# Gate scores carried by the residual's transposes, and expert outputs accumulated by DMA, in a convolution-attention and mixture-of-experts block

## What is computed

```python
t = t + ffn(ln_t(t))                       # t: (batch, 3136 tokens, 96)
# ffn(x):
scores = einsum('bsd,de->bse', x, gate_w) + gate_b
probs  = softmax(scores)
masked = probs * (top 2 of probs);  masked = masked / (sum(masked) + 1e-9)
h = gelu(einsum('bsd,edh->ebsh', x, w1) + b1)      # hidden 384
y = einsum('ebsh,ehd->ebsd', h, w2) + b2
out = einsum('bse,ebsd->bsd', masked, y)
```

## Time and profile before

| | us |
|---|---|
| three runs | 895.98, 898.64, 900.95 |
| median | 898.64 |
| span of the profiled execution | 894.8 |
| rest(0), 77 to 190 | PE busy 84.0 of 113.0 |
| round 1, 190 to 392 | PE 183.2, DVE 164.7 of 202.0 |
| round 2, 392 to 597 | PE 180.8, DVE 159.3 of 205.0 |
| round 3, 597 to 781 | PE 166.7, DVE 119.5 of 184.0 |
| last experts, 781 to 894.8 | PE 105.2, ACT 97.7 of 113.8 |

### The profile page before, as it was taken

One profiled execution on the slowest core, in us unless ns is written; L12 is line 12 of the kernel. 1 busy time (PEld: TensorE's weight loads), 2 busy tenths in 40 slices (PEclk: granted clock), 3 DMA queues, 4 the chain that ended last, 5 costly groups with the idle time before them and its releaser, 6 DMA issues.

```text
span 894.8 us, 10704 instructions
## 1 busy us (share of the span) xinstructions
PE 775.4 (87%) x3304; PEld 514.3 (57%) x3304; DVE 670.5 (75%) x1397; ACT 396.8 (44%) x726; POOL 322.5 (36%) x184
## 2 busy tenths in 40 slices
PE   2899779759997898988997798989996998999996
PEld 1454445645664456655664455755663556588885
DVE  6789769899896487878896587899882354667775
ACT  2322412424555107542555106544542134599995
POOL 2000700007777001127677002148897011234443
PEclk9998979559998899998999799999997996999998
DMA  9103401201232001261132001151422000221111
GB/s 179 44 0 108 108 1 54 55 34 39 91 103 79 7 4 36 82 160 39 60 127 83 8 0 39 47 133 42 148 72 78 0 25 16 87 70 55 62 55 31
DMA packets 17312, 55.12 MB, mean 62 GB/s; under 512 B 5008, under 2 KB 8720, under 8 KB 15216
## 3 DMA queue, kind: packets, MB, share of 16 engines
q1 hardware_dynamic: 12656, 39.90, 15.8%
q10 hardware_dynamic: 1536, 9.84, 3.3%
q0 software_dynamic: 3072, 4.82, 2.1%
HBM read 35.07 MB, written 14.65 MB: 56 GB/s over the span
## 4 chain that ended last, share of the span: by engine, by line
PE 51%; DVE 23%; POOL 11%; issue 7%; ACT 3%; DMA 3%; DVEq 0%; ACTq 0%; SPq 0%; POOLq 0%
PE py L615 10%; POOL big L1215 8%; PE pd L555 7%; DVE query L919 6%; PE pa L430 4%; PE ph L470 4%; PE pd L535 3%; POOL x L1225 3%; PE pd L578 3%; PE ph L630 3%; PE ph L631 2%; PE ph L632 2%; DVE key_area L919 2%; DVE big L919 2%; PE ph L653 2%
## 5 line engine op out<-in xcount | busy, mean ns | idle before, releaser
L1225 POOL TENSOR_TENSOR x<-x,ye 96x448 f32<-96x448 f32 x112 | 240.1, 2144 | 464.8 <-DVE ye L1143 461.3
L830 ACT ACTIVATE hid<-ph,b 128x448 f32<-128x448 f32 x252 | 159.0, 633 | 263.8 <-PE ph L632 261.0
L615 PE MATMUL py<-hid,w 128*96 128x448 f32 x504 | 241.0, 560 | 31.5 <-DVE ye L1143 24.4
L630 PE MATMUL ph<-x_hi,w_hi 96*128 (+1 forms) x252 | 169.7, 673 | 0.0
L1143 DVE SCALAR_TENSOR_TENSOR ye<-py,b,gate_all 96x448 f32<-96x448 f32 x112 | 75.3, 677 | 53.0 <-PE py L615 25.3
L615 PEld LDWEIGHTS py<-hid,w 128*96 128x96 f32 x504 | 82.1, 168 | 55.8 <-DVE ye L1143 16.6
L1215 POOL DMA_INDIRECT big<-value_table,rows x64 | 77.3, 1208 | 88.4 <-DMA value_table<-xT 69.2
L631 PE MATMUL ph<-x_lo,w_hi 96*128 (+1 forms) x252 | 94.8, 376 | 0.0
L632 PE MATMUL ph<-x_hi,w_lo 96*128 (+1 forms) x252 | 94.3, 374 | 0.0
L919 DVE SCALAR_TENSOR_TENSOR big<-xpad,conv_w,big 96x3136 f32<-96x3136 f32 (+1 forms) x28 | 90.0, 3215 | 4.7 <-issue 4.3
L919 DVE SCALAR_TENSOR_TENSOR query<-xpad,conv_w,query 96x3136 f32<-96x3136 f32 (+1 forms) x28 | 93.1, 3324 | 0.5
(11 more groups left out here) (136 smaller groups left out, 1089.8 us busy)
## 6 DMA issues: line engine op xcount, KB each, us to landing
gate_all<-gate_rows SPq DMA_DIRECT2D x56, 336.0 KB, 3.1
value_table<-xT ACTq DMA_DIRECT2D x8, 1176.0 KB, 7.2
xs<-in_x SPq DMA_DIRECT2D x4, 1176.0 KB, 8.5
x<-in_x SPq DMA_DIRECT2D x4, 1176.0 KB, 7.9
x<-x SPq DMA_DIRECT2D x4, 1176.0 KB, 6.9
out<-x SPq DMA_DIRECT2D x28, 168.0 KB, 2.0
big<-value_table,rows POOLq DMA_INDIRECT x64
big<-in_w SPq DMA_DIRECT2D x1, 576.0 KB
```

Source lines behind the costliest of these rows:

```text
L615: nc.tensor.matmul(py[e % 2][0:C, 0:GPIX], w2[:, c, :], hid[:, k % 3, :], start=(j == 0), stop=(j == CPE - 1)).then_inc(hid_used, 1)
L630: nc.tensor.matmul(bank, w1_hi[:, cols], xh[:, px], start=True, stop=False)
L830: nc.scalar.activation(hid[:, k % 3, :], ph[k % 2][:, 0:GPIX], ACT.Gelu, bias=b1[:, k % NCH:k % NCH + 1]).then_inc(hid_act, 1)
L1225: ins = p.tensor_tensor(r, r, ye[:, e, :], ALU.add)
```

## The change

1. **Scores with the transposes.** In `x1T` PE multiplies each tile of the residual by `ident_gate`, the identity with four more columns: `gate_w` less the mean of each of its columns. So a tile comes out as 96 channels and 4 raw scores (400 columns a bank instead of 384). The 112 matmuls L578 go. DVE makes the scores with two small operations (`rstd`, then `gate_b`) right behind the normalisation.
2. **Split of the normalised tokens.** `x1c` goes to the two DVE banks `pd`; ACT copies a bank to the high part, DVE subtracts it from the same bank for the low part and so frees the bank. The copy through `xc` and the cast L1083 go. The token tensor of this stage is no longer `xT` but lies in `big`.
3. **Expert outputs.** POOL issues an accumulating DMA (`x1 += ye`) for each output in place of the addition, and waits until it has landed before the next.
4. **Order.** `x1c` no longer has chunks between its groups, `exp` and `gateT` come earlier in the table, `normalise_off` runs with `no_turn`, and the loops of PE, ACT and DVE over rounds 1 and 2 are written out.
5. At the start, PE multiplies `gate_w` by a matrix of 1/96, and DVE subtracts.

```diff
-ROUND = [..., ("x1c", 66, 4, 12), ("score", 71, 0, 13),
-         ("exp", 74, 0, 4), ("gateT", 79, 0, 9), ("offc", 79, 0, 0), ("offs", 82, 0, 0), ...
+ROUND = [..., ("x1c", 66, 0, 12), ("exp", 70, 0, 0), ("gateT", 77, 0, 12), ("offc", 79, 0, 0), ("offs", 82, 0, 0), ...
-              ("x1c", 67, 2, 10), ("score", 72, 3, 10), ("exp", 77, 0, 4), ("gateT", 82, 0, 6), ("end", 84, 0, 1)]
+              ("x1c", 67, 0, 10), ("exp", 70, 0, 0), ("gateT", 78, 0, 12), ("end", 84, 0, 1)]
@@ PE, head
+                nc.tensor.matmul(py[0][0:C, 0:EXPERTS], mean_of, gate_w[:, :], start=True, stop=True).then_inc(gate_mean, 1)
@@ PE, rest
-                    transposes(bank, [x[:, (GRP * g + k) * TP:(GRP * g + k + 1) * TP] for k in range(GRP)], C, TP).then_inc(act_full, 1)
+                    for k in range(GRP):
+                        last = nc.tensor.matmul(bank[0:TP, k * XC:(k + 1) * XC], x[:, (GRP * g + k) * TP:(GRP * g + k + 1) * TP], ident_gate[:, :], start=True, stop=True)
+                    last.then_inc(act_full, 1)
...
-                channels_back(b, "x1c", x1_normed, x1_normed_act, before_x1c)
-                for g in range(NG - 3, NG):
-                    if g == NG - 1:
-                        chunks_to(plan.at("score"))
-                    last = scores(g)
-                last.then_inc(dve_full, 1)
+                for g in range(NG):
                     chunks_to(plan.at("x1c", g))
+                    ...
+                    bank = dve_bank(b, "x1c", g)
+                    transposes(bank, [x1T[:, GRP * g + k, 0:C] for k in range(GRP)], TP, C).then_inc(dve_full, 1)
@@ PE, ACT, DVE
-            with pe.Fori(0, BATCH - 2) as b:
+            for b in range(BATCH - 2):
@@ ACT, x1c
-                    empty(b, "x1c", g, xc[:, g * GPIX:(g + 1) * GPIX], C, GPIX)
+                    i, full = dve_job(b, "x1c", g)
+                    act.wait_ge(dve_full, full)
+                    nc.scalar.activation(xh[:, half(b) + g * GPIX:half(b) + (g + 1) * GPIX], pd[i][0:C, 0:GPIX], ACT.Copy).then_inc(x_high, 1)
@@ DVE, rest
+                link(v.tensor_tensor(sc[:, :, :], x1T[:, :, C:XC], full(rstd[0:TP, :]), ALU.mult))
+                link(v.tensor_tensor(sc[:, :, :], sc[:, :, :], gate_b..., ALU.add))
+                link(v.tensor_reduce(mx[:, :], sc[:, :, :], AX.X, ALU.max))
+                v.tensor_tensor(sc[:, :, :], sc[:, :, :], full(mx), ALU.subtract).then_inc(score_ready, 1)
                 if with_head:
                     dve.wait_ge(x1_normed_act, (b + 1) * (NG - NORM_DVE))
-                    normalise_off(b + 1, turn)
+                    normalise_off(b + 1, no_turn)
@@ DVE, split_x
-                        dve.wait_ge(act_done, acted(b, "x1c", g))
-                        link(v.tensor_copy(xh[:, to], xc[:, px]))
-                        v.tensor_tensor(xl[:, to], xc[:, px], xh[:, to].bitcast(f32), ALU.subtract).then_inc(x_split, 1)
-                        turn(0.9)
+                        dve.wait_ge(x_high, b * NG + g + 1)
+                        v.tensor_tensor(xl[:, to], pd[dve_job(b, "x1c", g)[0]][0:C, 0:GPIX], xh[:, to].bitcast(f32), ALU.subtract).then_inc(dve_done, 1)
@@ DVE, outputs_to
-                        dve.wait_ge(ye_summed, b * OUTPUTS + done[0] + 1)
+                        wait(dve, ye_summed, 16 * (b * OUTPUTS + done[0] + 1 - EXPERTS))
@@ POOL, sum_group
-                    ins = p.tensor_tensor(r, r, ye[:, e, :], ALU.add)
-                    ins.then_inc(ye_summed, 1)
-                    pool.wait_ge(ye_summed, EXPERTS + i * EXPERTS + e + 1)
+                    pool.dma_start(r, ye[:, e, :], accum_op=ALU.add).then_inc(ye_summed, 16)
+                    pool.wait_ge(ye_summed, 16 * (i * EXPERTS + e + 1))
```

More of the change, by code:

```diff
@@ L57 @@
 ACT_REST = (jobs("valT", NG) + jobs("xT", NG) + jobs("xc", NG) + jobs("mix", QUARTERS) + jobs("offT", 2)
-            + jobs("x1T", NG) + jobs("keyT", 2) + jobs("x1c", NG) + jobs("gateT", 1) + jobs("offc", 2))
+            + jobs("x1T", NG) + jobs("keyT", 2) + jobs("gateT", 1) + jobs("offc", 2))
 DVE_HEAD = jobs("offs", 1)
-DVE_REST = jobs("kv", QUARTERS) + jobs("y", NY) + jobs("score", 1) + jobs("offs", 1)
-HEAD_STEPS, FIRST_REST_STEPS, REST_STEPS = 71, 134, 154
+DVE_REST = jobs("kv", QUARTERS) + jobs("y", NY) + jobs("x1c", NG) + jobs("offs", 1)
 CHUNKS = NG * NCH
@@ L291, in job @@
             last = [j for j in rest if j not in head]
-            static = isinstance(b, int)
             if (name, g) not in head:
-                order = last if static and b == BATCH - 1 else rest
+                order = last if b == BATCH - 1 else rest
                 i = order.index((name, g)) + len(head)
-            elif static and b == 0:
+            elif b == 0:
                 i = head.index((name, g))
@@ L299, in job @@
                 i, b = rest.index((name, g)) + len(head), b - 1
-            return i % 2, b * len(rest) + i + 1
-        assert len(ACT_REST) % 2 == len(DVE_REST) % 2 == 0
+            i += b * len(rest)
+            return i % 2, i + 1
         def first(b):
-            return isinstance(b, int) and b == 0
+            return b == 0
         def act_job(b, name, g=0):
@@ L562, in rest @@
                 chunks_to(plan.at("x1T"))
+                if first(b):
+                    pe.wait_ge(gate_centred, 2)
                 for g in range(NG):
@@ L571, in rest @@
                 chunks_to(plan.at("x1c"))
[L572 to L591 removed]
+                for g in range(NG):
+                    chunks_to(plan.at("x1c", g))
+                    if g < NORM_DVE:
+                        pe.wait_ge(x1_normed, b * NORM_DVE + g + 1)
+                    else:
+                        pe.wait_ge(x1_normed_act, b * (NG - NORM_DVE) + g - NORM_DVE + 1)
+                    bank = dve_bank(b, "x1c", g)
+                    transposes(bank, [x1T[:, GRP * g + k, 0:C] for k in range(GRP)], TP, C).then_inc(dve_full, 1)
                 chunks_to(plan.at("gateT"))
@@ L842, in _ @@
             rest(0, True, PLAN, lambda number: None)
-            with act.Fori(0, BATCH - 2) as b:
+            for b in range(BATCH - 2):
                 gelus_to = experts(b)
@@ L892, in statistics, with norm_tokens @@
                 turn(1.9)
-            def norm_tokens(b, name, back, eps, stats, normed, turn):
+            def norm_tokens(b, src, name, back, eps, stats, normed, turn):
                 for g in range(NG):
@@ L1070, in rest @@
                     turn(0.0, "keyT")
-                norm_tokens(b, "x1T", "x1c", LN2_EPS, x1_stats, x1_normed, turn)
+                norm_tokens(b, x1T, "x1T", "x1c", LN2_EPS, x1_stats, x1_normed, turn)
+                full = lambda m: m[:, :].rearrange("p (t o) -> p t o", o=1).to_broadcast([TP, NT, EXPERTS])
+                link(v.tensor_tensor(sc[:, :, :], x1T[:, :, C:XC], full(rstd[0:TP, :]), ALU.mult))
+                link(v.tensor_tensor(sc[:, :, :], sc[:, :, :], gate_b[:, :].rearrange("p (o e) -> p o e", o=1).to_broadcast([TP, NT, EXPERTS]), ALU.add))
@@ L1094, in rest @@
-                dve.wait_ge(dve_done, dved(b, "score"))
-                link(v.tensor_reduce(mx[:, :], sc[:, :, :], AX.X, ALU.max))
-                turn(0.8, "exp")
-                v.tensor_tensor(sc[:, :, :], sc[:, :, :], full(mx), ALU.subtract).then_inc(score_ready, 1)
+                        dve.wait_ge(x_high, b * NG + g + 1)
+                        to = slice(half(b) + g * GPIX, half(b) + (g + 1) * GPIX)
+                        v.tensor_tensor(xl[:, to], pd[dve_job(b, "x1c", g)[0]][0:C, 0:GPIX], xh[:, to].bitcast(f32), ALU.subtract).then_inc(dve_done, 1)
@@ L1098, in rest @@
+                split_x(range(SPLIT_FIRST))
                 split_x(range(SPLIT_FIRST, NG))
+                turn(5.0)
                 for e in range(EXPERTS):
@@ L1128, in rest @@
                 turn(0.0, "end")
-                assert not with_head or n[0] == (FIRST_REST_STEPS if first(b) else REST_STEPS), n[0]
             def experts(b):
@@ L1193, in _ @@
             rest(0, True, no_turn)
-            with dve.Fori(0, BATCH - 2) as b:
+            for b in range(BATCH - 2):
                 outputs_to = experts(b)
```

74 lines of the change are left out of this document (31 added, 43 removed).

## The result

The changed kernel takes 928.67 us (median of 925.77 to 930.62), the kernel before beside it 897.31: a ratio of 1.033 (1.029 to 1.038). The profiled execution has a span of 926.4 against 894.8, 31.6 more. I had forecast 897.6, and 912 as the upper end. Single executions of one kernel lie up to some ten us apart with TensorE's granted clock, and the ratios here leave out the few that lie over 1.5 per cent above the kernel's fastest.

The account below looks back on a forecast made before the run. Neither PE nor DVE is full: DVE waits for POOL's gather early in a round, PE is late behind x1c. Terms +0.6 +1.5 -4.3 +1.4 -3.6 +3.4 = -1.0 give span 893.8, plus 3.8 is 897.6 us; range 886 to 912.

Parts of the forecast that it names:

- Head and rest(0): Start and rest(0), ahead of round 1: small matmul +0.3, rest(0) nothing, wider x1T columns the remainder; together +0.6 us.
- x1T term: Wider columns of x1T, counted only as the rest of the +0.6 us for the start and rest(0).
- Taps, gather and weighting ahead of x1c: Rounds 1 and 2 before x1c: shorter taps (-2.2, -1.6), gather -0.4, weighting L1037 -2.3, an output moved -0.6.
- x1c: Rounds 1 and 2: PE waits for banks DVE frees only behind normalise_off, and its clock drops; +7.0 and +6.3 us.
- The loop's turn: Between rounds 1 and 2: writing the loop out removes DVE's 4.33 us idle, nothing else waits there; -4.3 us, once.
- Gather and round 3: Round 3: taps -2.0, gather -0.4, two landings instead of additions +2.1, x1c without normalise_off -3.3; sum -3.6 us.
- Last experts: Last expert part: landings of 3.3 hide under outputs every 3.66 until the end; +3.4 us (2.5 to 4.1).
- x: Time of one accumulating DMA on POOL: taken as 3.3 us, between 3.0 and 3.8; an addition takes 1.12.
- C: Rival, last experts: accumulations waiting for each landing fall behind the outputs; 908 us at 4.0 each, 922 at 4.5; chance 0.15.
- B: Rival, x1c: costs less, as PE's clock stays at 2.4 GHz or DVE splits earlier; 888 us (886 to 891); chance 0.18.
- E: Rival, rounds: taps don't shorten without additions, so -5.8 us is gone; 903.4 us; chance 0.04.
- D: Rival, three rounds: taps hold POOL's DMA descriptors, so the gather starts 2.0 us later; 904.6 us; chance 0.13.

Follow-up runs that it names:

- run 3: Changed kernel with DVE's split of the seven groups moved ahead of the layer norm for the next image's offsets: 912.70 us, ratio 1.016.
- run 2: Kernel before with accumulating DMAs and the loops of rounds 1 and 2 written out: 885.46 us, ratio 0.987.
- run 8: Kernel before with written-out loops and accumulating DMAs, measured once more on another chip: 890.22 us, ratio 0.987.
- run 1: Changed kernel with additions back on POOL in place of the accumulating DMAs: 909.87 us, ratio 1.012.
- run 5: Changed kernel with additions back on POOL and the split ahead of the offsets' layer norm: 896.02 us, ratio 0.996.
- run 10: Kernel before with scores folded into x1T and loops written out; additions on POOL and x1c as before: 887.63 us, ratio 0.987.

## Why the prediction was wrong, by its steps

- **Head and rest(0)**, +0.6: measured +1.3, which says little, since output 0 comes anywhere from 202.8 to 208.5 in the profiled executions of all runs. The x1T term ("the rest being the wider columns") failed by its size: four columns more are not 4 per cent, but a second instruction for each tile, 0.87 instead of 0.41 a group, and it was left out of the rounds.
- **Taps, gather and weighting ahead of x1c**, -5.5 and -4.9: measured -1.1 and -1.6. The durations were right (3.47 and 1.52), the step from them to time was wrong, 4.4 and 3.3 us. "This comes back where DVE is on the path" and "3.3 in place of 4.26" took each accumulation in the clear; one stood beside the value's table and landed after 10.7, so the gather was no earlier, and behind the weighting DVE waited for PE.
- **x1c**, +7.0 and +6.3: mechanism right, shown by run 3; the size was +9.8 (0.2 to 10.0) and +9.6. The working put the end of `normalise_off` at 360.9, which its own terms don't give (360.46 + 2.86 less 0.85 and 0.68 is 361.8); measured 364.85. Too small were the start (x1T, 2.3 later), the scores' four small steps and an output ahead of the layer norm (1 to 2), and the pace of the banks (1.17 a group, as told).
- **The loop's turn**, -4.3: wrong both ways. Alone the written-out loops give 12 to 16, since waits in a loop cost all along it: the row 256.31 carried "[0.21 <-DVE query L919]", and I read past it. In the changed kernel the turn gave only 1.7, since "nothing else waits there" was false: the gates landed late, and DVE waited 3.40 for them.
- **Gather and round 3**, -3.6: measured +4.1. The step "two landings of 3.3 stand in place of additions" took the accumulation's clear time. Output 11's accumulation was issued 11.2 after the output was ready, so the gather and all behind it moved.
- **Last experts**, +3.4: measured +12.6. The failing step is "the chain 3.3 is under 3.66". From issue to issue it is 3.6 undisturbed, 3.92 on the mean. I had x as issue to landing and left out the 0.3 until the next issue, and I bounded it by transfers that stood alone. Why the mean is 3.92 here and 3.79 and 3.69 in runs 2 and 8 is open.
- **Rivals.** C names the mechanism: a mean of 3.92 in a chain that began 2.0 late gives 812.4 + 27 x 3.92 + 3.3 = 921.6, as seen. B is refuted: the granted clock was 0.50 behind the wait. So is E: taps do shorten, only the time isn't gained by it. D is refuted for accumulations, whose issues beside taps take 0.79 and follow each other in 3.6 where nothing else moves. For the gather's own issues its mechanism is seen: those that meet a tap last until about 0.9 behind its end, as well as the next two rows. In the changed kernel none in the rounds takes over 1.1, but none of the first ones met a tap. Before, round 3, with no addition ahead; then run 8, round 1 (its tap runs until 264.09):

```profile
663.41 3.80 POOL L1215 DMA_INDIRECT big<-value_table,rows  x1 [0.30 <-issue]
...
262.91 2.12 POOL L1215 DMA_INDIRECT big<-value_table,rows  x1 [2.86 <-DMA x<-ye]
```

  The price of one landing: the estimate of 2.4 us by the fit of the Trainium skill (DMA: Bandwidth & Descriptors, "Anatomy of one DMA — SWDGE (gpsimd) path") is under the lowest landing here, 3.2.

The span missed the sum by 32.6 us: 0.7 in the head, 7.7 ahead of x1c in rounds 1 and 2, 6.1 in x1c, 2.6 at the turn, 7.7 in round 3 and 9.2 in the last part, less 1.4 between rounds 2 and 3.

Set against the written-out loops (884.4), the change costs 44, made up so: 18.8 the accumulations (most of them in the last image), about 14 the split behind the layer norm (runs 1 and 5), about 11.6 the rest, of which x1c through `pd` with its lower clock is the larger part and the fold (run 10) 3 at most. By the ratios, which take out the chips, the three are 19, 15 and 8, together 42. The parts hold for undoing them in this order; put alone into the kernel before, the accumulations cost 1. How the last part is shared is open: a kernel with x1c through `pd` and separate scores was not tried.

## What to carry to other kernels

- A wait for a DMA's landing on a path is priced by what else is in flight there, and by its time from issue to next issue. List the large transfers of each stretch before putting a small DMA in place of an engine's operation.
- A shorter instruction gives time only if its engine is the one that others wait for at the next meeting. Here 5 us of shorter taps and weighting ended in waits for a gather and for PE; follow the saving to the next wait before it enters the sum.
- An instruction that frees a bank is as late as the last thing ahead of it on its engine. When a bank's emptying goes from one engine to another, read the new engine's queue at that place first.
- Undo the parts of a bundle one by one. The only part that gained clearly by itself was the one that seemed a side matter, the loops written out.
